# Four graph-attention layers: layer 0's features times their factors on GpSimd instead of VectorE, and its per-head maxima by one transpose and a small product

## The reference, cut to what matters

```
h  = relu(layernorm(x))
Wh = (h @ W).reshape(B, N, 4, 64)                  # 4 heads of 64 features
s_src, s_dst = Wh . a[:, :64], Wh . a[:, 64:]      # one score per node and head
e  = leaky_relu(s_src[i] + s_dst[j], 0.2), masked by adj
x  = x + elu(softmax_j(e) @ Wh)
```

## Time and profile before

| | us |
|---|---|
| median of 3 runs (lowest, highest) | 2835.07 (2833.32, 2835.57) |
| profiled execution | 2838.34 |
| its span, first to last instruction | 2836.5 |
| PE busy in the span | 2793.0 (98%) |
| VectorE (DVE) busy | 2454.7 (87%) |
| ScalarE (ACT) busy | 2281.5 (80%) |
| GpSimd (POOL) busy | 648.3 (23%) |
| DMA | 15 GB/s on average |

### The profile page before, as it was taken

How to read it: one execution, slowest core, us unless ns; L and a number is a source line. 1 busy time by engine, 2 the same in 40 slices (tenths; PEclk the granted TensorE clock), 3 DMA queues, 4 the chain that set the end, 5 groups by cost and what they waited for, 6 DMA issues and landing times.

```text
span 2836.5 us, 63430 instructions
## 1 busy us (share of the span) xinstructions
PE 2793.0 (98%) x23704; PEld 2492.5 (88%) x23704; DVE 2454.7 (87%) x6405; ACT 2281.5 (80%) x6079; POOL 648.3 (23%) x1051
## 2 busy tenths in 40 slices
PE   7999999999999999999999999999999999999996
PEld 7888889888998898898898888889988989888885
DVE  6898888898888988888988888988889888889875
ACT  5788878888878888888888788788788888887785
POOL 4122122221122221122221122221122211222111
PEclk9999999999999999999999999999999999999998
DMA  2000000000000000000000000000000000000000
GB/s 83 9 9 9 16 16 16 16 1 17 16 16 17 16 2 16 16 16 16 8 9 16 16 16 16 1 16 16 16 16 16 2 16 16 16 16 9 2 9 15
DMA packets 16785, 41.83 MB, mean 15 GB/s; under 512 B 5344, under 2 KB 7392, under 8 KB 16480
## 3 DMA queue, kind: packets, MB, share of 16 engines
q1 hardware_dynamic: 16480, 37.77, 3.8%
HBM read 20.99 MB, written 16.78 MB: 13 GB/s over the span
## 4 chain that ended last, share of the span: by engine, by line
PE 92%; DVE 5%; ACT 2%; issue 1%; SPq 0%; DMA 0%; POOL 0%; POOLq 0%; DVEq 0%
PE bank L597 48%; PE bank L695 23%; PE bank L729 8%; PE bank L683 4%; PE bank L647 4%; PE bank L816 1%; PE bank L671 1%; DVE R L920 1%; PE bank L767 1%; DVE Z L1015 1%; PE bank L773 1%; DVE oTlo L1021 0%; DVE R L1006 0%; PE bank L706 0%; DVE hT2lo L878 0%
## 5 line engine op out<-in xcount | busy, mean ns | idle before, releaser
L695 PE MATMUL bank<-hw,R 128*128 128x257 f32 x3072 | 722.0, 383 | 1.4 <-ACT hw L1241 1.2
L695 PEld LDWEIGHTS bank<-hw,R 128*128 128x128 f32 x3072 | 565.4, 191 | 86.9 <-issue 8.3
L1422 POOL TENSOR_TENSOR rs<-ve,mhalf 128x4 f32<-128x4 f32 x128 | 140.6, 1098 | 1830.2 <-DVE ve L863 1746.1
L920 DVE SCALAR_TENSOR_TENSOR R<-bank,E,mask_ne 128x512 f32<-128x512 f32 x640 | 452.3, 743 | 3.0 <-PE bank L683 2.2
L597 PE MATMUL bank<-wfc_hi,oThi 128*128 128x256 f32 (+1 forms) x1024 | 298.8, 292 | 0.0
L597 PE MATMUL bank<-wfc_hi,oTlo 128*128 128x256 f32 (+1 forms) x1024 | 288.5, 282 | 0.0
L597 PE MATMUL bank<-wfc_lo,oThi 128*128 128x256 f32 (+1 forms) x1024 | 288.5, 282 | 0.0
L729 PEld LDWEIGHTS bank<-hw,R 128*64 128x64 f32 x8192 | 251.0, 138 | 32.4 <-issue 29.2
L729 PE MATMUL bank<-hw,R 128*64 128x65 f32 x8192 | 269.0, 224 | 0.1
L1220 ACT ACTIVATE Z<-bank,rs 128x258 f32<-128x258 f32 (+1 forms) x384 | 176.0, 478 | 47.4 <-PE bank L597 46.5
L597 PEld LDWEIGHTS bank<-wfc_hi,oThi 128*128 128x128 f32 x1024 | 194.1, 190 | 1.0
(11 more groups left out here) (293 smaller groups left out, 8415.1 us busy)
## 6 DMA issues: line engine op xcount, KB each, us to landing
x<-in_x_dram SPq DMA_DIRECT2D x32, 512.0 KB, 3.6
out_dram<-x SPq DMA_DIRECT2D x31, 512.0 KB, 2.6
R<-in_adj_dram SPq DMA_DIRECT2D x2, 512.0 KB, 7.6
Z<-in_L_gnn_mlp_w_dram SPq DMA_DIRECT2D x2, 512.0 KB, 5.6
O<-in_L_gnn_W_fc_dram SPq DMA_DIRECT2D x1, 1024.0 KB, 7.1
out_dram<-x SPq DMA_DIRECT2D x4, 128.0 KB, 1.8
R<-in_L_gnn_W_dram SPq DMA_DIRECT2D x1, 256.0 KB, 4.0
R<-in_L_gnn_W_hand_dram SPq DMA_DIRECT2D x1, 256.0 KB, 6.6
```

The costliest lines, as they stand in the source:

```text
L695: ins = e.matmul(bk[:, 0:257], P[:, j, i * 128:(i + 1) * 128], hw[:, j, 0:257], start=(j == 0), stop=(j == NBLK - 1))
L920: e.scalar_tensor_tensor(P[:, t, :], bank_of(b, "row", p)[:, :], m["E"][:, 1, h, j:j + 1], mask[:, j, :], ALU.max, ALU.mult).then_inc(up(" ...
L1422: e.tensor_tensor(m["rs" + z][:, :], m["ve" + z][:, :], mhalf[:, :], ALU.pow).then_inc(up("rs", b), 1 if l == 1 else 3)
```

## The change

The features' multiplication moves from `vector_batch` to `pool_batch`. It becomes 16 operations of 128x64 in four steps, one step a head, each operation a `tensor_scalar` with the factor as a scalar of each partition. `hw0` counts 16 instead of 4, and the product of head h waits for its own four.

The maxima: `top(0)` makes one transpose of `tm` (128x4 in, 4x128 out); VectorE takes the maximum over 128 values on 4 partitions; in a new step `top(0)` transposes the four results, broadcast to 128 columns, against a 4x4 identity (128x4 out); VectorE's operations for `A` read that from PSUM, in a new step of their own. The bank is held until `A` is there, where it was free after the maximum. `top` of the other attentions stays one transpose.

At loading, the small DMAs of the score vectors count on the same semaphore as the weights of their group, so that the first users of the weights of groups 2, 4, 5 and 6 wait for these DMAs too.

All of `TURNS` but SP's string is new. PE has one more step a batch, VectorE three fewer, GpSimd four more. Where the new order puts the steps, counted from the strings:

- Steady part, PE, between the two steps of `top(0)`: for batch 12 (lane 0) one step of `turn(2)` of batch 10, four transposes; for batch 13 (lane 1) three matmuls of `attf` and a `row`; for batch 14 (lane 2) four matmuls of `attend`.
- Steady part, VectorE, batch 12: four steps stand between `tm` and `T`, three of them low parts of batch 11 (L936); before there were three, two of them low parts.
- GpSimd, batch 12: `power(2)` of batch 10, heads 0, 1, 2 of batch 12, `power(3)` of batch 10, four `center0` and `power(0)` of batch 13, then head 3 of batch 12. In the other two lanes head 3 follows right on `power(3)`.
- GpSimd at the start: `center0` and `power(0)` of batch 0, low parts of group 1, `center0` and `power(0)` of batch 1, head 0 of batch 0, three low parts of group 2, head 1, one low part, heads 2 and 3.
- ScalarE at the start: the high parts of group 1 stand before the last two copies to `raw` of batch 0 and those of group 2 right behind these; batch 0's factors stand behind the eight `entry_sums` steps of batch 2 and one copy of transposed weights (before: right behind its `E`).
- PE at the start: `project` of batch 1 stands before batch 0's product of head 2; before, it stood behind the product of head 3. Two heads' products of batch 1 now stand before `turn(1)` of batch 0, which came first before.

```diff
-    "h": (5, 4), "raw": (5, 4), "sc": (5, 5), "TM": (5,), "E": (5, 3), "row": (8,),
+    "h": (5, 4), "raw": (5, 4), "sc": (5, 5), "TM": (5, 2), "E": (5, 3), "row": (8,),
-    "rowc": (1,), "hw0": (4,), "att0": (4, 4), "den0": (4, 2), "y0": (4,), "e0": (4, 2), "x0": (4, 2),
+    "rowc": (1,), "hw0": (4, 4), "att0": (4, 4), "den0": (4, 2), "y0": (4,), "e0": (4, 2), "x0": (4, 2),
-        + [("TM0", 0, "sc", (0, 1)), ("row", 0, "P", (0, 3))]
+        + [("TM0", 0, "sc", (0, 3)), ("row", 0, "P", (0, 3))]
...
@@ tensor_batch, top(l, nh)
-                for h in range(nh):
-                    i = e.transpose(bk[:, h * 128:(h + 1) * 128], m["tm"][:, h:h + 1].broadcast_to([128, 128]),
-                                    ident[:, :])
-                i.then_inc(up("TM", b))
+                if l == 0:
+                    e.transpose(bk[0:NH, 0:128], m["tm"][:, :], ident[:, :]).then_inc(up("TM", b))
+                    yield
+                    w.wait_ge(*at("sc", b, l, 1))
+                    e.transpose(bk[:, 128:128 + NH], m["T"][0:NH, 0:1].broadcast_to([NH, 128]),
+                                ident[0:NH, 0:NH]).then_inc(up("TM", b))
+                else:
+                    e.transpose(bk[:, 0:128], m["tm"][:, 0:1].broadcast_to([128, 128]), ident[:, :]).then_inc(up("TM", b), 2)
@@ tensor_batch, product of head h
-                    w.wait_ge(*at("hw0", b, j))
+                    w.wait_ge(*at("hw0", b, h, j))
@@ vector_batch, scores
-                v2 = bank_of(b, f"TM{l}")[:, 0:nh * 128].rearrange("p (h n) -> p h n", h=nh)
-                e.tensor_reduce(m["T"][:, 0:nh], v2, AXX, ALU.max).then_inc(up("sc", b))
+                bk, np = bank_of(b, f"TM{l}"), 128 if nh == 1 else nh
+                e.tensor_reduce(m["T"][0:np, 0:1], bk[0:np, 0:128], AXX, ALU.max).then_inc(up("sc", b))
...
-                Tb = m["T"][:, 0:nh].rearrange("p (h o) -> p h o", o=1).broadcast_to([128, nh, NBLK])
+                yield
+                w.wait_ge(*at("TM", b, l, 1))
+                Tb = bk[:, 128:128 + nh].rearrange("p (h o) -> p h o", o=1).broadcast_to([128, nh, NBLK])
@@ vector_batch
-            for n in range(NBLK):
-                wb = hv[:, n, :, 64:65].broadcast_to([128, 4, 64])
-                e.tensor_tensor(hv[:, n, :, 0:64], rv[:, n], wb, ALU.mult).then_inc(up("hw0", b))
-                yield
@@ pool_batch, first steps
+            w.wait_ge(*at("E", b, 0, 2))
+            w.wait_ge(*at("raw", b, 0, 3))
+            if b >= LANES:
+                w.wait_ge(*at("att", b - LANES, 2, 3))
+            for h in range(4):
+                for n in range(NBLK):
+                    e.tensor_scalar(hvs[s][:, n, h, 0:64], rv[:, n, h, :], hvs[s][:, n, h, 64:65], None,
+                                    ALU.mult).then_inc(up("hw0", b))
+                yield
@@ loading
+        s_al = [new_sem("al0"), None, *s_wl[2:]]
+        WL = [16, 16, 48, 16, 48, 48, 48]
```

More of the change, by code:

```diff
@@ L80 @@
[L80 to L89, removed]
@@ new lines @@
+        "54345435443353333345544445435344444445543333443454433443434333434364644554444554556666555564645556445445454664"
+        "44444546555555655555555455456654454455465454554545444545475766555566556656666776666556655755765676576655755565"
+        "57766667666667556667675565566576655666655556565566666677677776777788776677676668867688666686868768777787787867"
+        "77677777776666788677667866777777666767697977887777887889999888897798889778778787997777778798888889888788888788"
+        "899877877887987878878787778787a8a99888899889989999aa9999889988a88a989a98a9988a88888aa99999a899999a9899a9a88988"
@@ new lines @@
+        "998a99889999888988988999999aa9aaaa9aaaabbaa99aa9a999bb9a9bb9999b9b9b9aaabaabaaabab9aa9aaaaaaa9999bab9aa9a9b99a"
+        "aaaaa999a9a9cacaabbaaaabbabbccccbbbbcacabbbcaabaababaccaaaaaabacbbbbbbcbbbbbbbaabbbbccbaabaabbacbababbababaaab"
+        "abadbdccbbbbccbbccbccccddccccbbccbbdbbdcbcdcbdccbbbdbbdbbdcccccdcccccdbcbccdcdbbbbcccbdccbbccccbbbbcbcbbcccccc"
+        "ddcddddcddddeeddccddcdccceecdceeccccecececdeddddedddeecdddcddddcdcddccdeecddcdceccddddddcccdcdcfdfddeeddddeede"
+        "effffeeeefdfdeeefddeddededffddddddedfeeeeeefeeeeeeeedeedeffeddeddeedfededeedededddededgegffeeeeffeeffeffffggff"
@@ new lines @@
+        "ffeeffeegeegfefgfegffeegeeeeeggfffffgeffffgffeffgfgeefeeffegffeeffffeeeefefeeffffffggfggggfgggghhggffggfgfffhh"
+        "fgfhhffffhfhfhfghgggghggghhfgggfgggggggffffghhfgggffhffggggggfffgfgfigggihhgggghhghhiiiihhhhigighhhigghgghghgi"
+        "igggggghgihhhhhhihhhhhhhhghhhigihgggghhhgihghghghhghggghghgjhjiihhhhiihhiihiiiijjiiiihhiihhjhhjihijihjiihhhjhh"
+        "hhjijiiijiiiiihjiihiijjhhihhiiihjiihhiiiihhhhihihhiiiiiijjijjjjijjjjkkjjiijjijiiikkijikkiiiikikikijjkjjjkjjjjk"
+        "kijjijjjjjjjiiiijkkijjijikiijjjjjjiiijijiljljjkkjjjjkkjkkllllkkkkljljkkkljjkjjkjkjlljjjjjjkljkkkkkkklkkkkkkkjl"
@@ new lines @@
+        "jkkklkjjjjkkkjlkjkjkjkkjkjjjkjkjmkmllkkkkllkkllkllllmmllllkkllkkmkkmlklmlkmllkkkmkkkkmmlllllmlllllmkllklmlmkkl"
+        "kkllkmllkkllllkkkklklkkllllllmmlmmmmlmmmmnnmmllmmllmllnnlmlnnllllnlnlnmnlmmmmnmmmnnmlmmlmmmmlmlmmllnmnlmmlmlnl"
+        "lmmmmmmlllmlmlomommnnmmmmnnmnnoooonnnnomomnnnommnmmnmnmoommmmmmnmonnnnnnnonnnnnnnmnnnomonmmnmmnnmonmnmnnmnmnmm"
+        "mnmnmpnpoonnnnoonnoonooooppoooonnoonnpnnponoponpoonnpnnnnnoppoooopooooopnonoopopnnonnonopoonnoooonnnnononnoooo"
+        "poopoppppoppppqqppooppopoooqqopoqqooooqoqoqoppqpppqppqpqpoppopppppppooopoqqoppopoqooppppppooopoporprpqpqppppqq"
@@ L311, in build @@
         s_wl = [new_sem(f"wl{n}") for n in range(7)]
-        s_al = [new_sem(f"al{n}") for n in range(7)]
+        s_al = [new_sem("al0"), None, *s_wl[2:]]
+        WL = [16, 16, 48, 16, 48, 48, 48]
         s_adj = [new_sem(f"adj{n}") for n in range(2)]
@@ L413, in tensor_group @@
             w.wait_ge(s_id, 1)
-            w.wait_ge(s_wl[n], 16)
+            w.wait_ge(s_wl[n], WL[n])
             if g in (1, 5):
```

215 lines of the change are left out of this document (102 added, 113 removed).

## The result

The changed kernel takes 2848.32 us (median of 4 runs, 2847.89 to 2850.36) where the kernel before takes 2834.83 beside it (4 runs). The ratio is 1.0048, with an interval of 1.0036 to 1.0061: slower by 13.5 us. The forecast was 2831.7, and the range ended at 2842. The profiled execution took 2848.75 us, its span is 2846.7.

The account below looks back on a forecast made before the run. The prediction took PE, busy 98% of the span, as the bound, other engines counting only where PE waits. PE -7.0, new wait +1.6 and start +2.0 sum to -3.4, forecasting a median of 2831.7 us, range 2823 to 2842.

Parts of the forecast that it names:

- PE's term: PE's transposes for the maxima: four replaced by two save 0.22 us a batch, -7.0 us in all; bounds -10.2 and +4.5.
- the sign of the shapes: In the trace of PE, 0.3 us or more a transpose would show that narrow transposes change the array's shape.
- The rival of the shapes: Narrow transposes on PE change the array's shape, 0.36 us a batch; PE's term +4.5, total 2843.2 us; chance 0.10.
- The new wait: PE's second transpose waits for VectorE's maximum: 0.15 us in each of 11 batches, +1.6 us; bounds 0 and 7.7.
- The rival in which the wait eats the gain: PE's wait for the maximum takes 0.6 us in 11 batches, 6.6 us, leaving -0.4, 2834.7 us; chance 0.17.
- VectorE: VectorE loses 62 us of multiplications and long maxima, off the path: between 0 and -2.7 us, counted 0.
- Cost 0: GpSimd gains 512 operations of 0.5 us, 256 us, hidden by the distance to the product and gaps around `pow`: 0.
- The rival in which GpSimd fails: GpSimd's operations take over 1.8 us or hold up VectorE, so PE waits: above 2850 us; chance 0.02.
- The start: Batch 0's head 0 is ready later on GpSimd: taken as +2 us, high end +8.8, low end 6.8 us of lost work.
- The rival of the start alone: At the start all 8.8 us of GpSimd's later head 0 show: +3.4, 2838.5 us; chance 0.08.
- The end and the late stretch: The end of the kernel is in layers that don't change: 0.
- more won: Maximum never late, and the start gains about 2 us as PE keeps its clock: -9, 2826 us; chance 0.25.

Follow-up runs that it names:

- the kernel with the steps in the gaps: Kernel before with only the multiplication moved to GpSimd, old order, each head's step in an idle gap of GpSimd: 2834.78 us, ratio 0.9998.
- the bare splice: Kernel before with only the multiplication moved to GpSimd, old order, each head's step some 6 us ahead of its product: 2844.23 us, ratio 1.003.
- The mended kernel in the old order: Both parts in the order of the kernel before, with full-size second transpose and GpSimd's steps in its idle gaps: 2840.13 us, ratio 1.0016.
- both transplants of the old start: Changed kernel with full-size second transpose, steps before 250 us, or before 110 us, put in the old order: 2843.81 us and 2843.25 us.

## Why the prediction was wrong

**PE's term failed: -7.0 came out as -1.9, and it is the largest loss that an experiment took away.** I priced the second transpose at 0.10 us by L767, which moves 2 columns but over 128 rows. With 4 rows it takes 0.34, more than the 0.3 that the prediction had named as the sign of the shapes. Taken out by the full-size transpose it gave back 6.8 us of 13.5 (5.0 by the distances in the traces). Six of the changed kernel's seven runs had a mean granted clock of 0.993, against three of eight with the full-size transpose, so what lies above 5.0 may be the clock's; that is not shown. The rival of the shapes had the mechanism, at 10%, with a wrong count: it charged both transposes with two changes of 0.09 each. In fact the first one costs nothing extra and the second 0.23 in all. So the rival's price of 0.36 us a batch was too high; its total, 2843.2, was too low all the same, for its other terms were the forecast's.

**The new wait**, +1.6, was too high for the planned order as a wait (0.4 us, once) and too low for the old order (2.9 us of idle time, 11 times, and 5.6 us by the distances in the middle alone). The rival in which the wait eats the gain had the right place, and the wrong form. But it misled me to price only the visible wait. The chain to `E` is longer in every batch, and an order either waits for it or pays elsewhere to cover it: the maxima alone, at full size, cost 6.5 us net of 7 us saved.

**VectorE**: the 62 us fewer came out as 41 of busy time, in which operations that overlap count once. Summed one by one over the trace, its operations took 62.6 us less (2803.9 and 2741.3). Single operations grew, such as the low part of `hT2` (L1070 before, L1071 after) from 706 to 758 ns, but it takes 761 in the kernel with the new order alone, where GpSimd multiplies nothing, and 704 with the multiplication on GpSimd in the old order: it goes with the order and not with GpSimd's traffic. Zero was right for the time: with 39 us less on VectorE the kernel with the steps in the gaps is no faster.

**GpSimd**: the operation's time was right. "Cost 0" looked only at the product that uses the features and at `pow`. I left out `presum`, which PE reads 1.5 us after it is done at 2600 us. The planned order found room (1.1 us of waits for it in the whole trace), the bare splice lost some 9 us. So in the changed kernel itself this step cost about nothing. The rival in which GpSimd fails did not come.

**The start**, +2, failed: +8.5 by 300 us. Batch 0's first product came at 36.09, inside the foreseen 33 to 38. The loss is not there but between 50 and 100 us, where PE waits for a low part of attention output 2.5 us, for a row of transposed weights 2.3, for a low part of `hT0` 1.1. The mended kernel in the old order has the same work and does not lose it, so it comes with the order and not with the operations. This sign of being wrong, a start that moves by more than 5 us, came true; the other, 8 us of idle time of PE in the middle, did not. The rival of the start alone had the size (8.8) by another mechanism, GpSimd's head 0 behind batch 1's `pow`. What the new order bought with it stays open, as both transplants of the old start gave it back, in part through falls of the clock at their seams.

**The end and the late stretch**, 0, failed: +4.7 between 2300 and 2700 us, +1.6 behind. The second transpose explains under 1 us of that. The old order there changed nothing. Why this stretch loses time stays open.

**The clock row misled the range.** I took the fall to 0.78 and 0.54 at 50 to 70 us for a property of the kernel that the change could lift, and gave "more won" 25% on it. The same kernel mostly runs without it: of 83 runs of the kernel before beside the experiments, 16 had a mean granted clock of 0.992 or 0.993 and took 2837.03 to 2839.83; the others had 0.994 or 0.995 and took 2836.9 at most. The trace that I started from, with its mean at the edge (0.994), took 3.3 us more than the median, and the fall accounts for that: it stood 5.6 us behind the second trace at 70 us. What it seemed to offer at the start was not the change's to win.

The range had slips of its own. Its low ends add up to 2822, not 2823. Its end at 2842 has no sum behind it and lies below the 2843.2 of the rival of the shapes, although PE's high end (+4.5), the wait's (7.7) and the start's (8.8) were all written down and reach past 2855 together.

What is shown: the second transpose's shape; the column sums in the bare splice; that each part alone is no gain, mended or not; that in the old order the wait for T eats most of the work saved; that the new order is 5 to 8 us behind by 300 us, the lower figure without the falls of the clock, and that this start can't be exchanged by itself. What is not: what in the new order's start makes the engines late, and what costs 4.7 us from 2300 us on.

## What to carry to other kernels

Price a small matmul by its rows as well as its columns, and measure it between neighbours: fewer rows than the array has can cost more than a full-size one. In a kernel where PE is 98% busy and goes in order, replacing four cheap independent instructions by two dependent ones trades 0.2 us of work for a longer chain, and here the chain decided. Before giving a step to an idle engine, list everything which that engine hands on, with the time between its end and its use; the mean load says nothing of it. Read a wait of PE from the distance of starts as well as from the idle time, which showed half of it here. And profile the base twice before reading a single trace's start.

## What the runs showed of the hardware

A transpose of 4 rows against 128 columns sits 0.203 us behind the last 128-row transpose (usual 0.109) and the wide products behind it come 0.14 us later than behind a full-size one; together 0.23 us. Its weights were never loaded ahead of it (0.003 us at most, 32 times), those of full-size ones 0.08 to 0.23 us ahead in 23 of 32. One with 128 rows and 4 columns shows no such gap.

TensorE's clock can differ between executions of one program. In the first trace of before, in finer slices than the earlier trace rows:

```profile
50.00:55.00 5.00, 3.63 (x26) 2.96 (x26) 4.79 (x19) 3.17 (x10) 1.35 (x3) 1.00 0.00 0
55.00:60.00 5.00, 4.49 (x22) 4.49 (x22) 4.28 (x8) 3.79 (x12) 4.82 (x8) 0.55 0.01 3
60.00:65.00 5.00, 5.00 (x27) 5.00 (x25) 3.39 (x8) 2.81 (x6) 4.71 (x7) 0.50 0.00 0
```

After 5 us in which PE was busy for 3.63 the clock went from 2.4 to 1.2 GHz at 55.5 us, although PE was busy for 4.49 of the next 5. The second execution, busy for 3.26 of the same 5 us, kept 2.4 GHz there. It had been at 1.2 GHz for 3.4 us from 33.7 on, where the first had not. The long fall is worth 5 us, and nothing later gives it back before 2700 us; of the 5.6 us between the two traces of before at 70 us, 5.5 are left at 2700.
